# Preparing the first two tiles between the weight products of the last quarter, in one program part

## What is computed

```
K = 2.0 * jnp.einsum('hn,hnl->hl', Cs, jnp.exp(P)).real
y = irfft(rfft(u * mask) * rfft(K)) + u * mask * D ; x = x + y * mask
x = x + (x @ W.T + 2 * sum_e gate_e * (x @ A_e.T) @ B_e.T)   # top 2 of 8 experts
x = x + (x @ W2.T + 0.5 * (x @ A_lab.T) @ B_lab.T)
x = x + x @ (quantized(W3 + delta) + delta).T
```

## Time and profile before

| | us |
|---|---|
| median of three runs | 1074.34 (1074.09 to 1076.32) |
| profiled execution | 1073.91 |
| its span, first to last instruction | 1072.1 |
| PE busy, matrix products | 1016.0 (95%) |
| DVE, ACT, POOL busy | 850.5, 433.9, 295.7 |

### The profile page before, as it was taken

The page is one execution under the profiler, slowest core; times in us unless marked ns, Lnnn a source line. Parts: engine busy times, 40 slices in busy tenths (PEclk is TensorE's granted clock), DMA queues, the critical chain, the costliest instruction groups (busy, mean ns, idle before and its releaser), DMA issues.

```text
span 1072.1 us, 16635 instructions
## 1 busy us (share of the span) xinstructions
PE 1016.0 (95%) x4851; PEld 808.3 (75%) x4851; DVE 850.5 (79%) x1679; ACT 433.9 (40%) x851; POOL 295.7 (28%) x318
## 2 busy tenths in 40 slices
PE   3999999999979759999999999999999999999997
PEld 2554555988868648888888888888888888888885
DVE  5887988989992268888888888888888888888862
ACT  3222212222275335543544454445535443544441
POOL 2200422284442422223222322322232223223200
PEclk9999999999999879999999999999999999999999
DMA  9601010010001343545445444544454455445321
GB/s 257 155 20 59 20 39 1 3 38 1 1 0 20 53 78 70 88 86 100 76 80 100 86 83 76 104 79 88 80 104 74 85 93 93 80 76 104 63 40 40
DMA packets 317018, 74.95 MB, mean 70 GB/s; under 512 B 292978, under 2 KB 309554, under 8 KB 316986
## 3 DMA queue, kind: packets, MB, share of 16 engines
q1 hardware_dynamic: 316986, 74.56, 35.7%
HBM read 57.61 MB, written 16.91 MB: 70 GB/s over the span
## 4 chain that ended last, share of the span: by engine, by line
PE 63%; DVE 2%; ACT 1%; issue 0%; ACTq 0%; DVEq 0%
PE bank L1142 33%; PE bank L1132 10%; PE bank L1163 4%; PE bank L1114 4%; PE bank L1103 4%; PE bank L1123 4%; PE bank L1169 2%; PE bank L1153 1%; PE bank L1092 1%; ACT ZZ L1243 0%; PE bank L1147 0%; PE bank L1158 0%; DVE ZZ L1391 0%; DVE xT L1402 0%; DVE ZZ L1382 0%
## 5 line engine op out<-in xcount | busy, mean ns | idle before, releaser
L1068 POOL TENSOR_TENSOR Cl<-QC,Ch 128x256 fp32r<-128x256 f32 x32 | 37.3, 1167 | 468.1 <-ACT Ch L1234 468.1
L1252 ACT ACTIVATE SK<-ZZ 64x448 f32<-64x448 f32 x128 | 73.9, 577 | 216.0 <-DVE ZZ L1391 213.6
L1142 PE MATMUL bank<-Mh,x0l 128*128 128x512 f32 x512 | 160.9, 396 | 0.0
L1142 PE MATMUL bank<-Ml,x0h 128*128 128x512 f32 x512 | 160.6, 395 | 0.0
L1142 PE MATMUL bank<-Mh,x0h 128*128 128x512 f32 x512 | 160.4, 394 | 0.0
L1391 DVE SCALAR_TENSOR_TENSOR ZZ<-ZZ,coef 128x192 f32<-128x192 f32 (+1 forms) x256 | 121.7, 515 | 10.1 <-DVE ZZ L1382 0.2
L530 PE MATMUL bank<-E,A 128*128 128x512 f32 (+1 forms) x384 | 127.4, 492 | 0.0
L1142 PEld LDWEIGHTS bank<-Mh,x0l 128*128 128x128 f32 x512 | 96.2, 188 | 23.0
L1142 PEld LDWEIGHTS bank<-Ml,x0h 128*128 128x128 f32 x512 | 96.2, 188 | 22.6
L530 PEld LDWEIGHTS bank<-E,A 128*128 128x128 f32 x384 | 64.8, 194 | 62.5 <-issue 62.5
L1142 PEld LDWEIGHTS bank<-Mh,x0h 128*128 128x128 f32 x512 | 94.6, 188 | 18.4
(11 more groups left out here) (283 smaller groups left out, 1967.5 us busy)
## 6 DMA issues: line engine op xcount, KB each, us to landing
X<-in_x SPq DMA_DIRECT2D x256, 64.0 KB, 2.3
XT<-in_x SPq DMA_DIRECT2D x256, 64.0 KB, 2.3
out_x<-O SPq DMA_DIRECT2D x64, 256.0 KB, 3.2
toep<-kpad SPq DMA_DIRECT2D x128, 64.0 KB, 2.1
E<-in_L_cond_W SPq DMA_DIRECT2D x8, 512.0 KB, 6.8
W2s<-in_L_cond_W SPq DMA_DIRECT2D x8, 512.0 KB, 4.3
vq<-in_L_cond_weight SPq DMA_DIRECT2D x8, 512.0 KB, 3.4
LA<-in_L_cond_lora_A SPq DMA_DIRECT2D x8, 80.0 KB, 3.4
```

Of the source, the lines that this page charges most:

```text
L1142: pe.matmul(psO[nh][:, :], xs[:, c, :], ms[:, c, nh * BANK:(nh + 1) * BANK], start=(c == 0 and n == 0), stop=False)
L1252: act.activation(SK[ri * N:(ri + 1) * N, hh, :].rearrange("p (c b) -> p c b", b=B), ZZ[hh * N:(hh + 1) * N, :, ri, :], ACT.Copy).then_inc( ...
```

## The change

Everything is now in one program part. The preparation of tiles 0 and 1 stands in the queues of the job list between the products of the last quarter. On DVE, `read(mt)` holds a step back until product mt of that quarter is done. The steps that need the tables (state columns, expansions, kernel sums) stand from product 2 on. In detail:

- PE: state transpose of tile 0 after product 5, chunk states of tile 0 and `kern` (one bank, operands exchanged, 64 products of 32 x 4) after 6, the transposes of the kernel's values and of tile 1's states after 7, `within` and `from_states` of tile 0 after 8. Tile 1's follow product 9. The state transpose of tile 2 stands inside tile 0, which is now written out ahead of the loop.
- The last quarter's products use four banks (4 to 7) instead of six.
- ACT: one sine step after (`m`, 2, 4), one exponential of both halves after (`m`, 2, 6), the second sine step after (`a3`, 3, 3). State columns after product 2 instead of 0.
- The kernel's values are made with 32 positions on partitions and transposed to one row of 128 per channel, so `kpad` is stored in rows of 512 bytes.
- SP asks for the first x loads after (`a3`, 2, 3), and for tile 1's ahead of the stores to `kpad`.
- Buffers: x strips lie in QT's place, 1152 words apart instead of 128; Sl is stored there in rows of 112. To make room, `init_quarter` for quarters 1, 2, 3 stands after QT tiles 3, 4, 6 instead of 1, 2, 3. `A3lo` has 128 rows, and POOL zeroes 64 of them at the start; PE waits for that.

```
-    A3lo = place("A3lo", [R3, L], F32R)
+    A3lo = place("A3lo", [2 * R3, L], F32R)
...
+    strips = place("strips", [P, NC, EW], F32, at=at_QT)
+    xq, xT = (strips[:, :, n * P:(n + 1) * P] for n in (0, 3))
...
-                        if 0 < kt < QUARTERS:
-                            init_quarter(kt)
+                        if kt in (3, 4, 6):
+                            init_quarter((3, 4, 6).index(kt) + 1)
...
+                pool.wait_ge(ld_b3, 64)
+                pool.tensor_tensor(A3lo[R3:, :], A3raw[R3:, :], A3raw[R3:, :], ALU.subtract).then_inc(a3_pad, 1)
...
+            return bank[2 + n % 6 if n < M_LAST else 4 + n % 4]
...
+                    if j == ("m", LAST_Q, 5):
+                        state_transpose(0, first=True)
+                    elif j == ("m", LAST_Q, 6):
+                        for hh in range(HB):
+                            chunk_states(0, hh, first=True)
+                        kern()
+                    elif j == ("m", LAST_Q, 7):
+                        kern_transpose()
+                        state_transpose(1)
+                    elif j == ("m", LAST_Q, 8):
+                        for hh in range(HB):
+                            within(0, hh, first=True)
+                        for hh in range(HB):
+                            from_states(0, hh)
+                for hh in range(HB):
+                    chunk_states(1, hh)
+                for hh in range(HB):
+                    within(1, hh)
...
-                for level in range(len(LEVELS)):
+                for level in range(2, len(LEVELS)):
```

More of the change, by code:

```diff
@@ new lines, in chunk_states @@
+                def chunk_states(i, hh, first=False):
+                    pe.wait_ge(xl_done, HB * i + hh + 1)
+                    if hh == 0:
+                        pe.wait_ge(bl_done, i + 1)
+                    if hh == 1 and not first:
+                        pe.wait_ge(z_out, 2 * HB * i)
+                    for n, (w, p) in enumerate(PARTS3):
+                        last = pe.matmul(psZ[hh][:, 0:SB].rearrange("p (c b) -> p c b", b=B), (Bh, Bl)[w][:, hh, :],
+                                         (xh, xl)[p][:, 0:NC - 1, hh * B:(hh + 1) * B], start=(n == 0), stop=(n == 2))
+                    last.then_inc(z_done, 1)
@@ new lines, in within @@
+                def within(i, hh, first=False):
+                    if hh == 0:
+                        pe.wait_ge(toep_loaded, 16 * PARTS * (i + 1))
+                    if not first:
+                        pe.wait_ge(x0_done, HB * (i - 1) + hh + 1)
+                    for n, (w, p) in enumerate(PARTS3):
+                        last = pe.matmul(psY[hh][:, :].rearrange("p (c b) -> p c b", b=B), toep[:, hh, w, :],
+                                         (xh, xl)[p][:, :, hh * B:(hh + 1) * B], start=(n == 0), stop=False, skip_group_check=True)
+                    last.then_inc(t0_done, 1)
@@ L579, in _ @@
+                for hh in range(HB):
+                    chunk_states(1, hh)
+                for hh in range(HB):
+                    within(1, hh)
+                pe.wait_ge(m_lo, len(mno))
+                tile(0, True, True, True, first=True)
+                with pe.Fori(1, LAST - 2) as i:
+                    tile(i, True, True, True)
+                tile(LAST - 2, True, True, False)
+                tile(LAST - 1, True, False, False)
+                tile(LAST, False, False, False)
             @block.scalar
@@ new lines, in states_out @@
+                def states_out(i, heads, first=False):
+                    act.wait_ge(scan_step, SCAN_STEPS * (i + 1))
+                    if not first:
+                        act.wait_ge(sl_done, i)
+                    for hh in heads:
+                        for ri in range(2):
+                            act.activation(SK[ri * N:(ri + 1) * N, hh, :].rearrange("p (c b) -> p c b", b=B), ZZ[hh * N:(hh + 1) * N, :, ri, :],
+                                           ACT.Copy).then_inc(sk_done, 1)
@@ L701, in _ @@
                         act.wait_ge(m_full, n + 1)
[L702 removed]
+                        act.activation(hi, m_bank(n)[rows, 0:QO], ACT.Copy)
                         if n == 0:
@@ new lines, in _ @@
+                for hh in range(HB):
+                    x0_hi(0, hh)
+                states_in(1)
+                act.sem_inc(out_taken, 1)
+                tile(0, True, True, True, first=True)
+                tile(1, True, True, True, second=True)
+                with act.Fori(2, LAST - 2) as i:
+                    tile(i, True, True, True)
+                tile(LAST - 2, True, True, False)
+                tile(LAST - 1, True, False, False)
+                tile(LAST, False, False, False)
@@ L953, in _, with read @@
                         step(last)
-                last.then_inc(tab_cols, 1)
-                dve.wait_ge(tab_cols, 1)
+                last.then_inc(tab_pow, 1)
+                dve.wait_ge(tab_pow, 1)
+                def read(mt):
+                    dve.wait_ge(m_full, mno["m", LAST_Q, mt] + 1)
+                read(0)
+                for hh in range(HB):
+                    turn_q(0, hh, first=True)
                 tc = [P, H, PARTS]
```

1044 lines of the change are left out of this document (513 added, 531 removed).

## The result

| | before | after |
|---|---|---|
| median, us | 1074.99 (4 runs, 1074.09 to 1076.32) | 1050.30 (4 runs, 1048.61 to 1051.54) |
| profiled execution, us | 1073.91 | 1051.54 |
| span, us | 1072.1 | 1049.7 |

The ratio is 0.9768, with a 95% interval of 0.9748 to 0.9789: 24.7 us less by the medians and 22.4 by the profiled executions. The forecast was 1055, with a range of 1047 to 1062.

The account below looks back on a forecast made before the run. PE bounds the loop; idle time lies between product stage and loop. Tile 0 starting 22.0 us earlier, less 3.4 paid back in it, gives -18.6: 1073.9 to 1055.3, forecast 1055, range 1047 to 1062.

Parts of the forecast that it names:

- The start of the program: Program start to third quarter's end: PE gains 2.5 us early, but DVE runs late; third quarter ends 3.3 us later, 318.1.
- POOL's operation: Start of the program: one more 64x1024 POOL operation beside DVE's small steps costs DVE and PE 1.2 us (0 to 1.6).
- the early waits: PE's waits of 2.44 and 2.19 us after the second and third QT tiles shrink, gaining PE 3.7 us.
- ready at 109.5: Second quarter's buffer fill on ACT takes the fourth's old place, 110.06 to 111.98, moved 2.5 us earlier.
- DVE's 4.4 us: DVE's second-quarter rounding begins at 111.0, 4.4 us late; 1.4 taken back, so 3.0 us late (1.0 to 4.5).
- Rival 1: DVE isn't late at the fourth quarter's transposes, the fill's delay being hidden or taken back: 1051 us, chance 0.14.
- Ahead of the fourth quarter: With less ACT table work before the last evacuation, the fourth quarter's first product starts at 319.4, 2.6 us ahead of 322.02.
- The fourth quarter: Tile 0's preparation stands between its products without new waits; PE reaches tile 0's first Toeplitz product at 357.0.
- rival 2: POOL is too slow for its 13 more operations in the fourth quarter, delaying ACT's evacuations: 1062 us, chance 0.13.
- The Toeplitz load: In the fourth quarter PE waits 4.0 us (2 to 7) for Toeplitz blocks through DRAM, then runs at the low clock.
- Tile 0: Begins at 372.0, 22.0 us earlier, but pays back 3.4 us (0.4 to 5) through later scan, table load and state transpose.
- Rivals 3 and 4: 3: x strips' new distance slows every loop tile, 1077 to 1148, chance 0.04. 4: waits only change place, 1074, chance 0.02.

Follow-up runs that it names:

- the variant with both gains: Changed kernel with most of tile 0's table-dependent steps one product earlier in the fourth quarter, plus an extra exponential behind ACT's copy of the kernel sums: 1045.15 us, ratio 0.9719.

## Why the prediction was right, and where it was not

**Bound and place of the gain: right.** The gain lies between the fourth quarter and the loop, and in the loop nothing moved (21.00 us a tile).

**The start of the program: wrong in three terms.** POOL's operation cost 1.5 on DVE (1.2 forecast), and the 128-row products, which the sum left out, gave PE back more: the first QT tile starts at 27.81 instead of 29.03. Of the early waits the forecast took 3.7 us, without the low clock behind them; PE was 7.3 us earlier at the fourth QT tile (92.46 to 85.16). The step that failed then is "ready at 109.5": it moved the fill by 2.5 us, not by the 8 that PE was early, so that DVE's 4.4 us (3.0 in the sum) never arose. DVE began 1.0 us later (107.58), and had its fourth quarter ready 0.45 us earlier (286.55). Rival 1 came true in its mechanism: DVE isn't late. Its number, 1051, is nearer to 1050.3 than the forecast, and the weighing that gave it 0.14 rested on this one delay. Its sign, no wait of 3 to 5 us at the transposes, was a poor one: the changed kernel has 1.83, but six of the eight variants with the same instructions up to there have 3.7 to 5.6, with the low clock of the forecast behind it. They wait because PE is early, not because DVE is late. The forecast also had no wait at 234.82, which took 3.6 us of PE's lead in the changed kernel and up to 4.6 in the variants.

**Ahead of the fourth quarter: right mechanism, other time.** 313.92 where 319.4 was forecast. Of these 5.5 us, 5.4 are the delay above: the third quarter's last product ended at 312.7 (313.92 - 1.18), not at 318.1. The additions of 3.49 us released PE as reckoned (310.33 + 3.49 = 313.82), and the run with the sine step moved back shows it.

**The fourth quarter: one cost missing.** From its start to PE's arrival at the Toeplitz products: 354.90 - 313.92 = 41.0 us, forecast 37.6. The sums took 4.47 instead of 3.9, and the product behind them 6.7 instead of 3.5, at the low clock. The forecast took the sums' cost from the row of the other operand order, as if the order didn't matter. No other inserted step made a wait; rival 2 is out (the operations added to POOL's queue in the quarter took 0.6 to 0.75 us each).

**The Toeplitz load: right.** A wait of 3.14 (4.0 forecast, 2 to 7), and the low clock behind it. The landing was 1.3 us where 2.5 was taken.

**Tile 0: right mechanism, smaller.** It begins at 369.91 (368 to 377 forecast). 2.1 us given back (3.4), with a wait of 1.32 (2.0), no fall of the clock (1.0), and the table load as one part of it.

**Rivals 3 and 4:** no row of the loop moved, and tile 0 starts 24.1 us earlier.

The errors had both signs: -5.5 at the quarter's start, +3.4 in it, about 0 at the Toeplitz products (-0.9 and +0.9), -1.3 in tile 0, in sum -3.4 on the profiled execution (1055.3 to 1051.54 is -3.8). The 3.4 us too few in the quarter hide a good part of the 5.5 too many ahead of it, so that the number came so near is in part luck.

## What to carry to other kernels

A gain far ahead of a place that another engine sets is worth only the slack at that place: look up when the other engine has its input ready there, and cap all earlier gains by it, before working any of them out in detail. When a step's result travels through another engine and DRAM, follow its place in each queue on the way; in the one case tried here, moving it on all of them but one gained nothing. When an edit moves a buffer or an event, move it by the whole change of the engine that issues it, low clock included.

## What the runs showed of the hardware

- The clock fell with no idle time ahead, behind 2.2 to 4.8 us of products that hold 32 columns and move 4, in nine of ten profiles; in four profiles with 4 held and 32 moved, of the same count, it didn't. Why the tenth kept it stays open.
- PE's waits and the clock: at the fourth quarter's transposes it stayed at 1.00 behind waits of 1.63, 1.64, 1.83, 1.94 and 2.25 us, and was at 0.50 behind 3.70, 3.72, 3.87, 4.01 (twice), 5.07 and 5.63 (twice). There is no fixed length for all places: waits of 2.15 (at 235.43, 64 rows) and 2.19 were followed by a fall, and one of 3.34 (at 234.06, the variant with both gains) by 1.00. Nor is there one at the Toeplitz products: the clock was at or near 0.50 behind waits of 2.66, 3.14, 3.21 and 3.25 us, and at 1.00 behind 3.04, 3.26, 3.32 and 3.36.
- Products of 64 rows between products of 128 rows run farther apart than when all have 128. The changed kernel with 64 rows, and as it is, both at clock 1.00:

```profile
82.11 0.50 PE L724 MATMUL bank<-A3hh,B3s 128*128 128x512 f32 x1
82.54 0.50 PE L724 MATMUL bank<-A3lo,B3s 64*128 64x512 f32 x1
```

```profile
83.08 0.40 PE L728 MATMUL bank<-A3lo,B3s 128*128 128x512 f32 x1
83.32 0.41 PE L728 MATMUL bank<-A3hh,B3s 128*128 128x512 f32 x1
```

Starts are 0.43 us apart with 64 rows and 0.24 with 128: twice the rows, of which half are zeros, in little over half the time.
- By "What ACT_TABLE_LOAD costs" in the Trainium skill's "ScalarE: Activation LUTs" a switch of tables takes a drain of 1.38 us besides the load. The trace has the exponential at 384.09, right behind 382.80 + 1.28, and in the kernel before a load at 302.14 with no more than 0.01 us behind it: no such gap, in this case.
